# GpSimd waits for each four indirect transfers to land before it issues the next four

## The reference

```python
logits = x @ router_w.T
probs = softmax(logits, axis=-1)
top_w, top_idx = jax.lax.top_k(probs, TOP_K)            # TOP_K = 2, E = 8
w_te = einsum('tk,tke->te', top_w, one_hot(top_idx, E))
g = einsum('th,eih->tei', x, gate_w)
u = einsum('th,eih->tei', x, up_w)
h = silu(g) * u
y = einsum('tei,ehi,te->th', h, down_w, w_te)
```

## Time and profile before

| | |
|---|---|
| runs, median (lowest to highest) | 1310.29 us (1307.22 to 1310.85) |
| profiled execution, span from first to last instruction | 1400.9 us |
| granted TensorE clock, mean over the span | 0.933 |
| busy share PE / PEld / DVE / ACT / POOL | 88% / 52% / 64% / 50% / 24% |
| L1930 scatter, 64 transfers | 62.0 us busy, 968 ns each |
| reload of the slots (L1979), issue to landing, median | 3.9 us (into wA), 4.2 us (into arena) |
| L1943 gather, 64 transfers | 61.2 us busy, 957 ns each |
| traffic of the indirect transfers (queue q0) | 4096 packets, 8.40 MB, 2.0% of the 16 DMA engines |

### The profile page before, as it was taken

One profiled execution on the slowest core, in us unless ns is written; L12 is line 12 of the kernel. 1 busy time (PEld: TensorE's weight loads), 2 busy tenths in 40 slices (PEclk: granted clock), 3 DMA queues, 4 the chain that ended last, 5 costly groups with the idle time before them and its releaser, 6 DMA issues.

```text
span 1400.9 us, 23674 instructions
## 1 busy us (share of the span) xinstructions
PE 1230.8 (88%) x9158; PEld 722.7 (52%) x9174; DVE 902.1 (64%) x1863; ACT 696.8 (50%) x1678; POOL 335.6 (24%) x349
## 2 busy tenths in 40 slices
PE   7969768899848896699999999946899999999998
PEld 4536246667525663266666776722444332333665
DVE  4698534444627767477767677724657887887476
ACT  2464236766615540165555555422566666666621
POOL 1332450000260304621301041072223341210100
PEclk9998889999979895699999999977999999999999
DMA  8100213432010110231532337320132134000000
GB/s 238 36 1 1 68 38 99 123 111 63 20 45 4 48 47 27 88 114 58 153 108 87 107 115 208 102 61 21 25 73 68 30 92 92 2 3 28 2 8 23
DMA packets 71468, 92.41 MB, mean 66 GB/s; under 512 B 9846, under 2 KB 55670, under 8 KB 69766
## 3 DMA queue, kind: packets, MB, share of 16 engines
q1 hardware_dynamic: 67260, 82.50, 21.0%
q0 software_dynamic: 4096, 8.40, 2.0%
HBM read 62.10 MB, written 28.77 MB: 65 GB/s over the span
## 4 chain that ended last, share of the span: by engine, by line
PE 70%; issue 10%; DVE 9%; another core or an unknown queue 6%; ACT 3%; POOL 1%; DMA 0%; SPq 0%; DVEq 0%; ACTq 0%; POOLq 0%
PE psB L428 33%; PE psA L428 30%; PE psB L432 5%; PE psA L432 2%; ACT pbuf L1791 2%; DVE mx L1458 1%; DVE st L1166 1%; POOL slots_x L1930 1%; DVE arena L1086 0%; DVE pbuf L1187 0%; ACT arena L1672 0%; ACT pbuf L1705 0%; DVE pbuf L1179 0%; DVE arena L1092 0%
## 5 line engine op out<-in xcount | busy, mean ns | idle before, releaser
L1791 ACT ACTIVATE pbuf<-psA 128x512 f32<-128x512 f32 (+3 forms) x768 | 351.8, 489 | 258.2 <-PE psA L428 204.4
L1458 DVE TENSOR_REDUCE mx<-psA 128x1 f32<-128x512 f32 (+3 forms) x520 | 326.4, 660 | 104.8 <-PE psA L428 76.7
L428 PE MATMUL psA<-arena 64*64 64x128 f32 (+6 forms) x1504 | 198.3, 295 | 31.9 <-issue 17.6
L428 PEld LDWEIGHTS psA<-arena 64*64 64x64 f32 (+3 forms) x1504 | 111.0, 135 | 112.6 <-issue 54.7
L1705 ACT ACTIVATE pbuf<-psA,st,rq 128x128 f32<-128x128 f32 x256 | 113.5, 459 | 94.5 <-DVE st L1169 77.0
L428 PE MATMUL psB<-pbuf,arena 128*64 128x128 f32 (+4 forms) x1536 | 134.1, 394 | 17.8 <-ACT pbuf L1717 10.2
L428 PE MATMUL psA<-w_mdiagT,w_identb 128*128 128x128 bf16 x512 | 110.7, 223 | 0.0
L428 PE MATMUL psA<-arena,w 96*128 96x512 bf16 (+4 forms) x320 | 108.5, 395 | 1.4 <-issue 1.2
L1847 POOL CAST arena<-tF 16x512 bf16<-16x512 f32 (+2 forms) x24 | 14.5, 605 | 324.3 <-DVE tF L1467 251.9
L428 PE MATMUL psB<-xf,wA 128*128 128x128 f32 x624 | 88.6, 283 | 0.8 <-DVE xf L1324 0.8
L428 PE MATMUL psA<-w,arena 102*128 102x512 bf16 (+5 forms) x272 | 82.6, 338 | 1.2 <-ACT pbuf L1791 0.9
(11 more groups left out here) (317 smaller groups left out, 2242.9 us busy)
## 6 DMA issues: line engine op xcount, KB each, us to landing
wA<-in_moe SPq DMA_DIRECT2D x39, 576.0 KB
wA<-in_moe SPq DMA_DIRECT2D x39, 256.0 KB, 3.1
slots_x<-wA SPq DMA_DIRECT2D x20, 256.0 KB, 3.7
slots_y<-tH SPq DMA_DIRECT2D x18, 256.0 KB, 3.6
wA<-slots_x SPq DMA_DIRECT2D x15, 256.0 KB, 3.9
arena<-stack1k SPq DMA_DIRECT2D x4, 768.0 KB, 6.6
arena<-stack2k SPq DMA_DIRECT2D x8, 384.0 KB, 7.4
stack1q<-arena SPq DMA_DIRECT2D x4, 384.0 KB, 3.9
```

Of the source, the lines that this page charges most:

```text
L428: return pe.matmul(out, lhsT, rhs, start=start, stop=stop, skip_group_check=True)
L1458: dv.tensor_reduce(m[:, t, h:h + c], maxb(lay, b, n)("mx", lay, b, n)[:, 0:c * k].rearrange("p (c k) -> p c k", c=c), AX.X, ALU.max) \
L1791: ac.activation(pb(lay, b, s, j)[:, 0:T - q0_], scoreb("ex", lay, b, s, j)[:, 0:T - q0_], ACT.Exp, bias=0.0, scale=1.0) \
```

## The change

After every four indirect transfers GpSimd now waits until the semaphore that they count has reached the value that includes them, that is, until all four have landed.

```diff
@@ xt (scatter)
                         po.indirect_dma_start(Xs[lay], IndirectOffsetOnAxis(i, 0), tok[:, t * P:(t + 1) * P], None) \
                             .then_inc(*xs_in[b].up(lay))
+                    po.wait_ge(*xs_in[b].now())
                 tH.give(("tok", lay, b), xs_in[b].now())
@@ cmb (gather)
                         po.indirect_dma_start(tH(*u)[:, t * P:(t + 1) * P], None, Ys[lay], IndirectOffsetOnAxis(i, 0)) \
                             .then_inc(*yg_in[b].up(lay))
+                    po.wait_ge(*yg_in[b].now())
```

## The result

| | kernel before | changed kernel |
|---|---|---|
| median of the runs | 1310.57 us (4 runs, 1307.22 to 1311.64) | 1352.62 us (4 runs, 1344.25 to 1357.71) |
| ratio | | 1.0321, 95% interval 1.0278 to 1.0363 |
| profiled execution, span | 1400.9 us | 1355.9 us |
| its own time | not given | 1357.71 us |
| granted TensorE clock, mean | 0.933 | 0.942 |

The account below looks back on a forecast made before the run. TensorE was taken as the bound (70% of the chain), with profile holes absent from timed runs. Lateness 8.0 + 4.8 + 3.7 + 3.7 = 20.2 us, two thirds passed on as 14: 1310.3 + 14 = 1324 us, range 1306 to 1337.

Parts of the forecast that it names:

- The holes belong to the recorded execution: Transfer bursts: 94 us of idle TensorE and 84 us of unexplained chain exist only in the profile, not in timed runs.
- a timeline with the holes taken out: Four bursts: 20.1 + 23.0 + 15 + 30.0 = 88 us removed from the profiled span, leaving 1313 against 1310.3.
- the page on the record-writing block: Trainium skill, NOTIFIC overflow: the trace-record block holds producers back, which would fit holes only in a recorded execution.
- The price of a wait: GpSimd, behind each four transfers: 1.2 us per wait (1.05 to 3.0), one group of each scatter burst at 3.0.
- The covers of 2.2, 1.2, 7.7 and 4.7 us: Time burst results lie ready before use: layer 0 scatter, gather, layer 1 `rot` sum, gather; late by 8.0, 4.8, 3.7, 3.7.
- Two thirds are passed on: Whole kernel: of 20.2 us summed lateness 14 us lengthen the run, as other engines still have work and TensorE some idle time.
- Rival (3): All bursts: landings cost 3.0 us each, late by 65, two thirds of it 43: 1354 us; chance 0.04.
- Rival (2): Holes are real in timed runs; pausing slows the pace a fifth, holes shrink likewise: -18, 1292 us; chance 0.12.
- Rival (1): All waits hidden: GpSimd still early, each burst's lateness about 0, 1310 us; chance 0.19.
- Gaps of 1.3 to 1.7 us: Expected sign in the changed profile: GpSimd's gap behind every fourth transfer, with 0.30 us within a group.
- The reload of layer 0's tokens: Expected sign: SyncE's scatter reload later against the burst's start by 8 to 10 us, less what lost gaps give back.
- The profiled span did fall: Expected sign: span may fall while runs slow, since slower bursts may dig smaller holes; falling with the runs would refute the forecast.

Follow-up runs that it names:

- e6: Kernel before with each GpSimd wait one group late, up to eight transfers under way, on chip B: 1308.49 us beside 1308.41 (1.0003).
- e5: The changed kernel itself, all 32 waits, no further edit, beside the kernel before on chip B: 1352.02 us beside 1308.41 (1.0315).
- e17: The changed kernel itself, all 32 waits, no further edit, beside the kernel before on chip D: 1350.82 us beside 1413.43 (0.958).
- e16: Kernel before plus a small GpSimd power computation behind each four transfers, no wait, on chip D: 1342.75 us (0.951).
- e18: Kernel before plus a small GpSimd copy behind each four transfers, no wait, on chip D: 1407.37 us (0.9949).
- e11: Kernel before plus a wait behind every eighth transfer, 16 waits, on chip C: 1376.57 us beside 1406.49 (0.9794).
- e15: Kernel before with each GpSimd wait one group late, up to eight transfers under way, on chip D: 1415.71 us beside 1408.85 (1.0053).

## Why the prediction was wrong, step by step

- **"The holes belong to the recorded execution": failed.** The profiled run of e6 has no holes (span 1305.9, time 1307.71), and on chips A, C and D all 57 runs of the kernel before take 1401 to 1423 us. Holes go with the chip, as far as four chips show. What I built on it, a timeline with the holes taken out, was right for the level on which the result was measured, by the wrong reason, and so by luck. Recording alone brings no holes, as chip B shows. But every run of the experiments has a span on record, and whether executions on chips of the upper level would have holes without any recording wasn't tried. That these are the chips whose traces miss most of the transfers' update records leaves room for it, and the page on the record-writing block that I cited stays undecided.
- **The price of a wait: term too small.** 1.2 us held in the undisturbed scatters (1.24) but not in the gathers (about 1.5), and in the scatter of layer 1 two waits cost 4.2 and 1.9 where I had put one at 3.0. My delays ahead of the last landings were 10.2 + 6.0 + 11.4 + 8.4 = 36; the gaps of the trace make 10.4 + 7.5 + 14.0 + 10.5 = 42.4.
- **The covers of 2.2, 1.2, 7.7 and 4.7 us: failed in all but one.** Without holes (e6) TensorE waits 1.41 us for the first reloaded tokens and VectorE 4.59 us for the last gather of layer 0, so these two have no cover at all. The last `rot` sum ends at 543.40 and VectorE takes it at 549.25, a cover of 5.8 where I had 7.7. The last gather of layer 1 is issued at 895.07, lands some 2.5 us later and is taken at 898.78: 1.2. The rows of e6:

```profile
200.51 1.43 PE L432 MATMUL psB<-w_ident,wA 128*128 128x128 f32 x8 [1.41 <-DMA wA<-slots_x]
```

```profile
395.86 1.29 DVE L1346 TENSOR_TENSOR tH<-tH,top_w 128x512 f32<-128x512 f32 x2 [4.59 <-DMA tH<-slots_y,slot_i]
...
549.25 0.69 DVE L1422 TENSOR_TENSOR arena<-arena,psB 128x512 f32<-128x512 f32 x1 [1.19 <-PE psB L432]
...
898.78 1.28 DVE L1346 TENSOR_TENSOR tH<-tH,top_w 128x512 f32<-128x512 f32 x2
```

  I had subtracted whole holes from positions, although engines in a hole partly had work of their own. With 42.4 of delay and 7 of cover, in place of 36 and 15.8, the lateness is 35.4, not 20.2; the pair of e5 and e6 has the same 35.4 at the waiting engines.
- **"Two thirds are passed on": failed, and it was the wrong way to round.** The row that I named myself, TensorE 94% busy elsewhere, spoke for the whole. All of the 35 is passed on, and 8 more come on top (43.6 between the medians). My sum had no term for them. Five of them stand in the stretch behind the first scatter, at the lower granted clock; where the other 3 come from is open.
- **The rivals.** Rival (3) has the number (1354) but not the mechanism: landings cost 1.24 to 1.5, not 3.0. Rival (2), the holes are real, is what happens on the upper level, and it decides there as I wrote; but it sized the effect by pace (a fifth less). The waits remove them nearly whole (14.7 us of unexplained pieces are left in the chain of e17): the 105 us between the two levels come back, 43 are paid, and 62.6 remain. Rival (1) is closed by both traces.
- **What was to be seen.** 0.30 us within a group held. Gaps of 1.3 to 1.7 us held for most waits in the scatters (the others are 1.94 to 4.52), but for none in the gathers, where the next issue comes after 1.76 to 1.88. The reload of layer 0's tokens comes 10.0 us later against the burst's start (45.2 in e6, 55.3 in e5), as I had said. The profiled span did fall while the runs got slower. I had called that a sign of smaller holes. It was one of a profile from the upper level beside one from the lower.

No complete version beats the kernel before on the lower level. On the upper level the pause without a wait (e16, 1343 beside 1409) is the fastest seen, though its interval overlaps with that of the changed kernel there.

## What to carry to other kernels

Where a profile's span and the timed runs of one kernel differ by far, take it as two machines until a run shows its own span beside its own time, and forecast each level for itself; this change is 3% slower on one chip and 4% faster on another. A chain that an engine hardly appears in says nothing of how much more that engine may be given: ask how long its results lie unused before they are taken, in a trace without the disturbance, and pass on in full what exceeds it where, as here, TensorE is over 90% busy. A wait for landing costs the gap behind the issue less the 0.30 us that it replaces; to wait one group late cost nothing on the lower level and 0.5% on the upper.

## What the runs showed of the hardware that was not expected

- On three of four chips, while GpSimd writes descriptors of indirect transfers with gaps of 0.30 us, semaphore updates between the other engines come late, by 11 us in the hole looked at here. A break of 1.26 us after four transfers (e16) prevents nearly all of it, one of 0.37 us (e18) doesn't, and a wait after eight transfers (e11) does so only in part. On the fourth chip the same kernel has none of it. Why the chips differ is open.
- On the three chips with holes the traces miss most update records of the indirect transfers (435 of 2048 in e15, against 2036 in e6).
- GpSimd itself isn't held up in a hole: its issues keep their 1.26 us, and update records of its transfers go on, some three to a transfer.
